# Four V stores on another queue and a reciprocal one step later, in a fused attention kernel

## The chip, the cores and the metric

The kernel runs on one core of a Trainium2 chip. The metric is the device time of one execution in microseconds; the median of three runs of the kernel before is 1255.03 (1254.48 to 1257.87).

## What is computed

Thirty-two sequences of 32 tokens with 512 channels pass a fused block: attention over a paged key and value cache (16 pages of 32 tokens per sequence) and the sequence's own new keys and values, a long convolution whose kernel is computed from state space parameters, a linear layer with a LoRA of each sequence, and a feed-forward part with gated low-rank experts. The change touches attention alone:

```python
q = rope(rmsnorm(einsum('bsd,ed->bse', x, Wq)))        # 32 heads of 128
k = rope(rmsnorm(einsum('bsd,ed->bse', x, Wk)))        # 8 heads
v = einsum('bsd,ed->bse', x, Wv)                       # 8 heads
k_all = concat([k_cache[block_table], k]); v_all = concat([v_cache[block_table], v])
scores = einsum('bqhd,bkhd->bhqk', q, k_all) * SCALE   # cached keys past the length masked
o = einsum('bhqk,bkhd->bqhd', softmax(scores), v_all)
x = x + conv(o @ Wo)
```

## The kernel before, in words

The work is done in two halves of 16 sequences (`HALVES`, loop variable h on every engine). A half is, in order: the projections of V's first four heads, K, Q and V's last four heads, twelve blocks of four tiles (128 tokens by 512 columns, each tile three passes of split float32 products, `tile`); the passage, in which the last V block is computed between the last transposes of Q; attention; the output projection and what follows. Each engine runs its own program; the order on it is written out by hand and held by semaphores.

**New keys and values.** K and V of the new tokens go through DRAM (`kn_d`, `vn_d`), since attention needs them in another layout. ScalarE (ACT) copies a V tile out of PSUM into a stage and, for the last four tiles (`col` 1, `store_v`, line 704), waits for its own copy and issues the store from its queue (lines 711 to 715). The first four tiles (`col` 0) are stored by SP (line 456). The stage of the last four has two slots, so the copy of tile m waits for the store of tile m-2. Both queues count in `vn_out`.

**SP's queue.** SP issues nearly all loads in one fixed order: keys' pages of batch 0, weights, at line 510 a wait for the last projection block but one, the first 8 key pages of batch 1, V's 16 pages of batch 0 (line 523, with a wait every four pages), key pages 8 to 15 and the new keys of batch 1, the wait for all V stores (line 525), both batches' new values (line 480), V's pages of batch 1 (line 485), and then per batch 16 key pages (line 470), new keys (line 475), new values and 16 V pages.

**Attention.** A batch is one sequence with 8 key heads g; the four query heads of a key head times 32 tokens are the 128 rows of a step. A step of each engine, for head g:
- TensorE (`attend`): scores of g, with key and query split in two parts (lines 1084 to 1095; L1090 is the first matmul that takes the keys' remainder `kbuf_lo`; every fourth head takes whole float32 instead, lines 1072 and 1074), transposes of the probabilities of g-3 (line 1107) into PSUM bank 4, products with V of g-4 (line 1139). Twice per batch the new tokens follow (lines 1119 and 1149), so that L1149 marks half-batches of four heads.
- VectorE (`step`, line 1622): masked maximum of g (line 1636) with its accumulator read, copy of the transposed probabilities of g-3 from PSUM (line 1642), a wait for ScalarE's exponential of g, reciprocal of the row sum of g (line 1649), and for g 1 and 5 `lower_q` (line 1595), the remainder of the next four query heads. TensorE may not transpose into bank 4 again before the copy (`pt_main`).
- ScalarE: high part of the keys of g+2 (line 815), exponential of g with the row sum (line 856), copies.
- GpSimd (POOL), `lower_keys`: per head g the keys' remainder of g (line 630, three heads of four), then `scale_probs(g-2)` (lines 616 and 618), which waits for the reciprocal (`rinv_ready`) and makes the probabilities ready to be transposed. The order is fixed: the remainder of the next keys stands behind the scale of the head before.

## Time and profile before

| | us |
|---|---|
| median of three runs | 1255.03 |
| the profiled execution, its time | 1256.73 |
| its span, first to last instruction | 1254.8 |
| TensorE busy in it | 1228.1 (98%) |
| VectorE, ScalarE, GpSimd busy | 808.2, 788.1, 749.5 |
| mean DMA rate | 171 GB/s |

The granted TensorE clock was 1.000 over the whole span. Matmul busy times are modelled and overlap, so 98% says that TensorE seldom stands, not that it is at its peak. The profile's chain is followed back from the last instruction; "SPq" in it is SP's queue issuing DMAs, "issue" is time in which nothing that the profile shows was waited for. PEld is TensorE's load of weights, which runs ahead of the matmul that uses them.

### The profile page before, as it was taken

How to read it: one execution, taken by the hardware profiler on the slowest of the kernel's cores; microseconds unless marked ns; L12 is line 12 of the kernel's file. 1: busy time of each engine (PE TensorE's matmuls, PEld its weight loads, DVE VectorE, ACT ScalarE, POOL GpSimd, SP SyncE). 2: the span in 40 equal slices, each digit the busy share in tenths (PEclk: the TensorE clock that was granted, in tenths of full speed). 3: DMA queues.
4: the chain of work that ended last, by engine and by line, in shares of the span. 5: the costliest groups of instructions: out<-in, count | busy, mean ns of one | idle time of the engine just before them, and what ended most of it. 6: DMA issues, size and time to landing. Idle time of an engine off the chain costs nothing.

```text
span 1254.8 us, 28770 instructions
## 1 busy us (share of the span) xinstructions
PE 1228.1 (98%) x7378; PEld 1031.9 (82%) x7378; DVE 808.2 (64%) x1736; ACT 788.1 (63%) x2259; POOL 749.5 (60%) x884
## 2 busy tenths in 40 slices
PE   7999999999999999999999999999999999999998
PEld 6788888899999997865777888888999999888756
DVE  6976666667666778951459667666766676655422
ACT  5666677778777774432346666777777777744320
POOL 4343467888888875433233443788888888844320
PEclk9999999999999999999999999999999999999999
DMA  6524288998999955306135252998899999534300
GB/s 206 194 92 149 95 232 220 230 232 233 236 236 237 229 159 177 142 8 194 68 105 184 84 172 91 243 220 227 224 234 240 231 238 239 121 116 153 89 30 34
DMA packets 147978, 214.82 MB, mean 171 GB/s; under 512 B 24949, under 2 KB 119479, under 8 KB 142136
## 3 DMA queue, kind: packets, MB, share of 16 engines
q1 hardware_dynamic: 134792, 206.96, 60.2%
q10 hardware_dynamic: 13104, 6.94, 1.9%
q8 instruction: 30, 0.49, 0.2%
q14 instruction: 52, 0.43, 0.1%
HBM read 203.33 MB, written 10.49 MB: 170 GB/s over the span
## 4 chain that ended last, share of the span: by engine, by line
PE 74%; SPq 15%; issue 5%; DVE 3%; ACT 1%; DMA 1%; ACTq 0%; DVEq 0%
PE PS L1139 12%; PE PS L1107 6%; SPq L485 6%; SPq L470 6%; PE PS L1206 5%; PE PS L1197 5%; PE PS L1001 5%; PE PS L1203 5%; PE PS L1005 5%; PE PS L999 5%; PE PS L1149 3%; PE PS L1248 2%; PE PS L985 2%; PE PS L1072 2%; PE PS L1237 1%
## 5 line engine op out<-in xcount | busy, mean ns | idle before, releaser
L630 POOL TENSOR_TENSOR kv_parts<-kv,k_hi 128x544 fp32r<-128x544 f32 x192 | 258.4, 1346 | 59.9 <-ACT k_hi L815 59.7
L1139 PE MATMUL PS<-probT,kv 128*128 128x128 f32 x2048 | 270.3, 275 | 0.0
L590 POOL TENSOR_TENSOR ring_parts<-ring,kv_parts 128x512 fp32r<-128x512 f32 x96 | 126.0, 1318 | 209.9 <-ACT kv_parts L693 181.6
L1139 PEld LDWEIGHTS PS<-probT,kv 128*128 128x128 f32 x2048 | 248.8, 192 | 0.0
L856 ACT ACTIVATE ring<-ring,smin 128x544 f32<-128x544 f32 x192 | 142.9, 744 | 86.9 <-DVE smin L1636 86.6
L1642 DVE COPY probT<-PS 128x512 f32<-128x512 f32 x256 | 175.5, 686 | 5.4 <-PE PS L1107 5.4
L1636 DVE CUSTOM_DVE_ANT_0 ring<-PS,mask,rq 128x544 f32<-128x544 f32 x192 | 149.7, 780 | 38.2 <-PE PS L1095 28.7
L652 POOL TENSOR_TENSOR ring_parts<-ring,kv_parts 128x512 fp32r<-128x512 f32 x64 | 85.0, 1332 | 95.1 <-ACT kv_parts L906 95.1
L815 ACT ACTIVATE k_hi<-kv 128x544 fp32r<-128x544 f32 x192 | 124.6, 650 | 15.5 <-DMA kv<-k_new 9.6
L618 POOL TENSOR_SCALAR ring<-ring,rinv 128x512 f32<-128x512 f32 x192 | 133.1, 693 | 0.0
L1676 DVE TENSOR_TENSOR qo_parts<-qo,kv_parts 128x512 fp32r<-128x512 f32 x64 | 85.3, 1339 | 54.1 <-ACT kv_parts L914 51.5
L1107 PE MATMUL PS<-consts,ring 128*128 128x128 f32 x768 | 115.8, 273 | 3.2 <-DVE probT L1642 2.4
L616 POOL TENSOR_SCALAR ring<-ring,rinv 128x32 f32<-128x32 f32 x192 | 79.6, 415 | 62.3 <-DVE rinv L1649 62.3
L1649 DVE RECIPROCAL rinv<-rsum 128x1 f32<-128x1 f32 x254 | 41.6, 164 | 114.7 <-ACT ring L856 95.6
L999 PE MATMUL PS<-kv_parts 128*128 128x512 f32 x352 | 102.3, 411 | 3.1 <-ACT kv_parts L693 1.5
L1206 PE MATMUL PS<-qo_parts,kv_parts 128*128 128x512 f32 x256 | 101.9, 398 | 0.0
L1197 PE MATMUL PS<-kv_parts 128*128 128x512 f32 x256 | 101.9, 398 | 0.0
L1203 PE MATMUL PS<-kv_parts,ring_parts 128*128 128x512 f32 x256 | 100.2, 392 | 0.0
L906 ACT ACTIVATE kv_parts<-ring 128x512 fp32r<-128x512 f32 x64 | 40.2, 631 | 94.5 <-PE PS L1197 94.4
L1107 PEld LDWEIGHTS PS<-consts,ring 128*128 128x128 f32 x768 | 89.8, 140 | 8.1 <-DVE probT L1642 3.3
L1001 PE MATMUL PS<-kv_parts 128*128 128x512 f32 x352 | 95.2, 392 | 0.0
L1005 PE MATMUL PS<-ring_parts,kv_parts 128*128 128x512 f32 x352 | 94.8, 391 | 0.0
(218 smaller groups left out, 2743.9 us busy)
## 6 DMA issues: line engine op xcount, KB each, us to landing
kv<-in_kpages SPq DMA_DIRECT2D x512, 128.0 KB, 2.5
kv<-in_vpages SPq DMA_DIRECT2D x512, 128.0 KB
ring<-in_w SPq DMA_DIRECT2D x44, 1024.0 KB, 5.0
k_new<-kv ACTq DMA_DIRECT2D x16, 256.0 KB, 2.3
kv<-k_new SPq DMA_DIRECT2D x32, 128.0 KB, 2.5
kv<-v_new SPq DMA_DIRECT2D x32, 128.0 KB
kv<-in_xT SPq DMA_DIRECT2D x8, 256.0 KB, 5.2
ring<-in_w SPq DMA_DIRECT2D x8, 256.0 KB, 5.4
```

What stands on the lines that cost most here:

```text
L630: nc.gpsimd.tensor_tensor(kbuf_lo(par)[:, :, g, :], kbuf(par)[:, :, g, :], k_hi[:, e % 2, :].rearrange("p (j t) -> p j t", t=PSIZE), ALU.s ...
L856: nc.scalar.activation(a, a, ACT.Exp, scale=-1.0, bias=smin[:, g:g + 1], accum_out=rsum[:, g:g + 1]).then_inc(exp_done, 1)
L999: nc.tensor.matmul(dst, x_hi[:, c, ms], hi[:, c, :], start=(c == 0), stop=False)
L1001: nc.tensor.matmul(dst, x_lo[:, c, ms], hi[:, c, :], start=False, stop=False)
L1005: mm = nc.tensor.matmul(dst, x_hi[:, c, ms], lo[:, c, :], start=False, stop=(c == KC - 1))
L1107: mm = nc.tensor.transpose(PS[:, 2048 + c * P:2048 + (c + 1) * P], prob(g % PRING)[:, c * P:(c + 1) * P], ident)
L1139: mm = nc.tensor.matmul(PS[:, at:at + D], vbuf(bpar)[:, c, gg * D:(gg + 1) * D], probT[:, g % 2, c * P:(c + 1) * P], start=(c == 0 and a = ...
L1197: mm = nc.tensor.matmul(bank(c), whi[:, a, cs], ohi[:, a, :], start=(head == 0), stop=False)
L1203: nc.tensor.matmul(bank(c), w[:, cs], ohi[:, a, :], start=False, stop=False)
L1206: mm = nc.tensor.matmul(bank(c), whi[:, a, cs], o, start=False, stop=(head == HQ - 1))
L1636: V.tensor_tensor_reduce(prob(g % PRING)[:, 0:LK], PS[:, at:at + LK], mask[:, par, :], rq[:, par, g:g + 1], 3.0e38, ALU.add, ALU.min, smin ...
L1642: V.tensor_copy(probT[:, (g - 3) % 2, :], bank(4)).then_inc(pt_main, 1)
```

## The change

Two edits. First, the stores of V's last four tiles move from ACT's queue to SP's: three between the V pages of batch 0 (after pages 3, 7 and 11), the fourth behind the new keys of batch 1 and directly ahead of SP's wait for all V stores. `store_values` now serves both columns. Second, in VectorE's step the reciprocal of a row sum moves: the one of head g-1 stands behind the masked maximum of g and ahead of the copy, and `lower_q` stands behind the copy.

```diff
@@ SP @@
+                def store_values(col, m, order):
+                    sp.wait_ge(v_read, h * (2 * TILES) + col * TILES + order + 1)
+                    sp.dma_start(vn_d[ds(h * HB + 4 * m, 4), :, col * D:(col + 1) * D]
+                                 .rearrange("b (t a) d -> (b t) a d", a=GU),
+                                 v_stage(col, m).rearrange("p (a d) -> p a d", a=GU)).then_inc(vn_out[m % 2], 16)
+
+                for order, m in enumerate((2, 3, 0, 1)):
+                    store_values(0, m, order)
...
                     load_value_page(0, j, pages[j])
+                    if j % 4 == 3 and j < NPP - 1:
+                        store_values(1, j // 4, j // 4)
+                        sp.sem_inc(sp_past, 1)
...
                 load_key_pages(1, pages, 8, NPP)
                 load_new_keys(1, 1)
+                store_values(1, 3, 3)
                 for n in range(2):
                     sp.wait_ge(vn_out[n], 8 * KU * (h + 1))
@@ ACT @@
-                    if col == 0:
-                        return
-                    act.wait_ge(v_read, h * (2 * TILES) + TILES + m + 1)
-                    act.dma_start(vn_d[ds(h * HB + 4 * m, 4), :, D:2 * D]
-                                  .rearrange("b (t a) d -> (b t) a d", a=GU),
-                                  v_stage(1, m).rearrange("p (a d) -> p a d", a=GU))\
-                        .then_inc(vn_out[m % 2], 16)
@@ VectorE, step @@
+                    if g <= HK and not (first and g == 0):
+
+                        k = (g - 1) % HK
+                        dve.wait_ge(exp_done, s)
+                        V.reciprocal(rinv[:, k:k + 1], rsum[:, k:k + 1]).then_inc(rinv_ready, 1)
                     if not (first and g < 3):
                         dve.wait_ge(pt_ready, s - 2)
                         if not (first and g < 5):
                             dve.wait_ge(pv_done, s - 4)
                         V.tensor_copy(probT[:, (g - 3) % 2, :], bank(4)).then_inc(pt_main, 1)
-                    if first and g == 1:
-                        dve.wait_ge(exp_done, s)
-                        V.reciprocal(rinv[:, 0:1], rsum[:, 0:1]).then_inc(rinv_ready, 1)
-                    if g < HK and not (first and g == 0):
-
-                        dve.wait_ge(exp_done, s + 1)
-                        V.reciprocal(rinv[:, g:g + 1], rsum[:, g:g + 1]).then_inc(rinv_ready, 1)
-                        if g % GU == 1:
-                            nb, u = (b, 1) if g == 1 else ((b + 1) % HB, 0)
-                            dve.wait_ge(qhi_ready, h * (QUADS + 1) + b * UNITS + g // GU + 2)
-                            dve.sem_inc(dve_past, 1)
-                            lower_q(u, ds(nb * (HQ * SEQ) + u * GU * D, NS * D))
+                    if g < HK and g % GU == 1:
+                        nb, u = (b, 1) if g == 1 else ((b + 1) % HB, 0)
+                        dve.wait_ge(qhi_ready, h * (QUADS + 1) + b * UNITS + g // GU + 2)
+                        dve.sem_inc(dve_past, 1)
+                        lower_q(u, ds(nb * (HQ * SEQ) + u * GU * D, NS * D))
```

## Rows read from the trace of the kernel before

**Rows 1.** The page, part 4: shares of the span on the chain that ended last.

```profile
PE 74%; SPq 15%; issue 5%; DVE 3%; ACT 1%; DMA 1%; ACTq 0%; DVEq 0%
```

**Rows 2.** The chain in order of time, 146 to 240 us: start, length, what.

```profile
148.69 0.98 SPq L463
...
177.91 1.62 SPq L485
...
233.76 2.43 DMA kv<-k_new
```

**Rows 3.** The same chain, 773 to 925 us (half 1), where it leaves SP.

```profile
915.53 2.86 DMA kv<-k_new
```

**Rows 4.** Line 456, SP's stores of V's first tiles: issue to landing.

```profile
DMA to landing us min/median/max: 2.6/2.7/2.9
```

**Rows 5.** Line 712, ACT's stores of V's last tiles: issue to landing.

```profile
DMA to landing us min/median/max: 3.2/3.9/5.4
```

**Rows 6.** Timeline of SP, 171 to 182 us: start, length, line, operation, count.

```profile
171.76 1.52 SPq L480 DMA_DIRECT2D kv<-v_new  x2
```

**Rows 7.** Timeline of TensorE's matmuls, 146 to 182 us; in brackets idle time and releaser.

```profile
165.68 0.40 PE L1090 MATMUL PS<-kv_parts,q_hi 128*128 128x288 f32 x1 [0.64 <-POOL kv_parts L630]
```

**Rows 8.** Timeline of VectorE, 413 to 421 us.

```profile
415.40 0.78 DVE L1636 CUSTOM_DVE_ANT_0 ring<-PS,mask,rq 128x544 f32<-128x544 f32 x1 [0.44 <-PE PS L1095]
...
416.11 0.69 DVE L1642 COPY probT<-PS 128x512 f32<-128x512 f32 x1
417.10 0.16 DVE L1649 RECIPROCAL rinv<-rsum 128x1 f32<-128x1 f32 x1 [0.31 <-ACT ring L856]
417.50 0.56 DVE L1595 TENSOR_TENSOR q_lo<-qo,q_hi 128x384 fp32r<-128x384 f32 x1 [0.24 <-issue]
417.98 0.78 DVE L1636 CUSTOM_DVE_ANT_0 ring<-PS,mask,rq 128x544 f32<-128x544 f32 x1
...
418.68 0.68 DVE L1642 COPY probT<-PS 128x512 f32<-128x512 f32 x1
```

**Rows 9.** Timeline of POOL, 413 to 421 us.

```profile
415.55 0.29 POOL L616 TENSOR_SCALAR ring<-prob,rinv 128x32 f32<-128x32 f32 x1
415.81 0.70 POOL L618 TENSOR_SCALAR prob<-prob,rinv 128x512 f32<-128x512 f32 x1
417.46 0.67 POOL L616 TENSOR_SCALAR ring<-ring,rinv 128x32 f32<-128x32 f32 x1 [0.95 <-DVE rinv L1649]
...
418.77 1.34 POOL L630 TENSOR_TENSOR kv_parts<-kv,k_hi 128x544 fp32r<-128x544 f32 x1
```

**Rows 10.** Timeline of TensorE's weight loads, 404 to 424 us.

```profile
411.44 0.19 PEld L1090 LDWEIGHTS PS<-kv_parts,q_hi 128*128 128x128 f32 x1
...
414.76 0.19 PEld L1095 LDWEIGHTS PS<-k_hi,q_lo 128*128 128x128 f32 x1
...
416.98 0.47 PEld L1107 LDWEIGHTS PS<-consts,ring 128*128 128x128 f32 x4
...
419.48 0.42 PEld L1107 LDWEIGHTS PS<-consts,prob 128*128 128x128 f32 x4 [0.27 <-issue]
...
421.01 0.19 PEld L1090 LDWEIGHTS PS<-kv_parts,q_hi 128*128 128x128 f32 x1
```

**Rows 11.** Timeline of TensorE, line 1149: one per half-batch, far apart in attention.

```profile
250.64 1.02 PE L1149 MATMUL PS<-kv 128*128 128x512 f32 x2
...
260.13 0.59 PE L1149 MATMUL PS<-kv 128*128 128x512 f32 x1
...
461.31 1.02 PE L1149 MATMUL PS<-kv 128*128 128x512 f32 x2
...
1085.74 0.59 PE L1149 MATMUL PS<-kv 128*128 128x512 f32 x1
```

**Rows 12.** Timelines of VectorE and POOL, 147 to 185 us: `lower_q` beside a scale.

```profile
166.43 0.61 DVE L1595 TENSOR_TENSOR q_lo<-qo,q_hi 128x384 fp32r<-128x384 f32 x1
...
165.94 0.69 POOL L618 TENSOR_SCALAR prob<-prob,rinv 128x512 f32<-128x512 f32 x1
```

More of the change, by code:

```diff
@@ L453, in _ @@
             with sp.Fori(0, HALVES) as h:
-                for k, m in enumerate((2, 3, 0, 1)):
-                    sp.wait_ge(v_read, h * (2 * TILES) + k + 1)
-                    sp.dma_start(vn_d[ds(h * HB + 4 * m, 4), :, 0:D].rearrange("b (t a) d -> (b t) a d", a=GU),
-                                 v_stage(0, m).rearrange("p (a d) -> p a d", a=GU)).then_inc(vn_out[m % 2], 16)
+                def store_values(col, m, order):
[5 more added lines that the diff above has]
+                    store_values(0, m, order)
                 with sp.Fori(0, 2) as i:
```

## The prediction

> **What bounds the kernel now.** I read the page's chain first. By engine it gives TensorE 74% of the span and SP's queue 15% [rows 1]: most of the run is matmul after matmul, but a sixth of it is SP issuing DMAs. Where does that lie? The chain in order of time shows one block per half: from 148.69, when SP reads the page table, it runs through SP's issues without a wait and leaves SP only at 233.76, with the landing of batch 4's new keys [rows 2]; in half 1 the block ends at 915.53 [rows 3]. From the passage into attention, up to batch 4 (half 0) or batch 7 (half 1), **SP's issue sequence sets the end**: what ACT, POOL or TensorE win there is lost again waiting for the next keys, and what SP loses there, the end loses. Behind that block attention is TensorE's: its half-batches (four heads) follow each other at (461.31 - 250.64) / 22 = 9.58 us [rows 11], the short ones at 9.49 (260.13 - 250.64). At most 0.09 of 9.58 is to be won.
>
> **Part 1: V's last four tiles stored by SP.** ACT loses four DMA issues and the waits on its own copies. SP gains, per half, three stores between V pages, one store behind `load_new_keys(1, 1)`, four waits on `v_read` and three increments.
> - ACT's side. Its third wait and issue stand before the key copy of head 2, so POOL's remainder of those keys comes late and TensorE stands 0.64 us at L1090 [rows 7]. Without them that stall goes, and perhaps as much again two heads on: 0.6 to 1.3 us a half. It lies inside SP's block, so I put it at **0**; it counts only if SP's block doesn't (rival D).
> - SP's issues. Two issues of like length (three-dimensional, L480) took 1.52 us [rows 6], 0.76 each. Three stores in the page loop: 3 x 0.75 = 2.25 us. Their waits I put at nothing: each has four page issues ahead of it, in which ACT makes the next copy. Queued behind them are V's pages of batch 0, the new values of both batches and all later keys and pages.
> - SP's new wait. The fourth store stands directly before the wait for `vn_out`, which wants all stores landed. Today ACT has issued the last one before SP is through with the second batch's keys, and no wait shows there. Now SP sits out a landing: 2.6 to 2.9 us for the stores of the projection [rows 4], 3.2 to 5.4 for those of this passage [rows 5]. I take 3.2 plus 0.1 of reaction, the low end of the nearer row (same place, busy DMA, but one store and not four). The landing holds the store's own issue.
> - What may come back: SP's issues sometimes stall, 1.62 us at 177.91 against some 0.4 for its neighbours [rows 2]. A queue that drained during the wait should not stall so soon; between 0 and 1.25, I take 0.4.
> - Sum: 2.25 + 3.3 - 0.4 = 5.2 us a half, **10.4 in all**. Bounds: 2.25 + 2.6 - 1.25 = 3.6 and 2.25 + 4.0 = 6.3 a half, 7 to 12.5 in all.
>
> The Trainium skill (DMA: Bandwidth & Descriptors, Issuing engines are not separate DMA queues) says that issuing from several engines only saves the sequencer's time, usually small. By that rule alone the part would be four issues, 3.0 us a half, and the forecast 4.4 us lower; it leaves out the landing.
>
> **Part 2: the reciprocal one step later.** Today VectorE does the masked maximum (L1636) and the copy of the turned probabilities (L1642), waits 0.3 us for ScalarE's exponential of the same head and takes the reciprocal (L1649); at heads 1 and 5 `lower_q` (L1595) follows [rows 8]. After: maximum of head g, reciprocal of g-1 with no wait, copy, and `lower_q` behind the copy. Two consequences, in times of the half-batch that starts at TensorE's load of L1090 for its first head, 411.44, and whose next starts at 421.01 [rows 10].
> - The copy comes later by the reciprocal, X, and TensorE's next transposes wait for it. For head 1: load of L1095 414.76, maximum 0.64 later (415.40), copy 0.71 after that, 0.69 long, and 0.12 to the load (418.68 + 0.68 to 419.48, a case that had to wait) = 2.16 + X, while TensorE itself is there 2.22 us after 414.76 (416.98). The slack is 0.06; behind head 3 I take 0.08. X is between 0.08 (the reciprocal's 0.16 less the 0.08 by which neighbours overlap: 417.98 against 417.50 + 0.56) and 0.40 (417.10 to 417.50, waits included) [rows 8]. The waits now stand behind an instruction of 0.78 us, which hides them, so I take 0.08: at most 0.03 a half-batch.
> - POOL gets the reciprocal of head g a step later. Today it scales head 0 at 415.55, stands, gets head 1's at 417.46, and that scale's first instruction takes 0.67 where 0.29 is usual [rows 9]: `lower_q` runs at 417.50. The two take turns. The other order is at 166.43: `lower_q` started beside a scale that ended at 165.94 + 0.69 = 166.63, and itself ended at 167.04, 0.41 behind it [rows 12]. After the change **the scale of head 0 and `lower_q` meet each time**. `lower_q` would start 0.08 + 0.69 - 0.08 = 0.69 behind reciprocal 0; POOL's long scale instruction starts 0.36 + 0.26 = 0.62 behind it and is first. The chain: L1090 of the first head to L1095 of head 1, 3.32; maximum 0.64; reciprocal of head 0, 0.71; POOL starts, 0.36 (417.10 to 417.46); both scale instructions 0.96 (415.55 to 416.51); `lower_q`'s 0.41 less 0.08 overlap; maximum of head 2, 0.71; reciprocal of head 1, POOL 0.36; its scale 0.93; then, in POOL's order, the remainder of the next keys, 1.34; TensorE 0.05. Sum 3.32 + 0.64 + 0.71 + 0.36 + 0.96 + 0.33 + 0.71 + 0.36 + 0.93 + 1.34 + 0.05 = **9.71**. Today that remainder starts at 418.77 and ends 0.9 us before its load at 421.01, which hides it; afterwards POOL sets the pace, 9.71 against 9.58. In SP's block that is hidden again (SP is slower still); outside it are 22 half-batches and a rest in half 0 and (1085.74 - 915.53) / 9.58 = 18 in half 1 [rows 3, 11]: 40 x 0.13 = **5.2 us** (0 to 10, for 0.12 either way in a chain of eleven terms).
>
> The Trainium skill (SBUF — State Buffer, SBUF: two separate sides) calls the port pair of VectorE and GpSimd an exclusive lock, held for a whole instruction, against a VectorE operation with two SBUF inputs, which `lower_q` is. By that rule the trace agrees in both directions, and the rule speaks against this change.
>
> **Sum.** The profiled execution took 1256.7 (span 1254.8). 1256.7 + 10.4 + 5.2 = 1272.3; the median of the runs shown is 1.7 lower than the profiled one, so **1271 us**.
>
> **Rivals.**
> - A, the forecast, chance 0.42: both costs hold; 1265 to 1277.
> - B, 0.20: SP's cost holds, but `lower_q` gets in ahead of the long scale (0.07 decides). Then 0.7 of the chain goes, and TensorE stays the bound at 9.49 to 9.58, on average 2 us less: 1255 + 10.4 - 2 = 1263 (1258 to 1268). For it: the margin is thin. Against: POOL's 0.36 is a steady figure and X can only be larger.
> - C, 0.12: POOL's cost holds, SP's is absorbed but for 1 us: 1255 + 5 + 1 = 1261 (1257 to 1264).
> - D, 0.20, **faster**: SP's additions vanish and attention doesn't suffer. It is decided by batch 2's keys: if they land no later than today in spite of four stores and a landing, because pages wait for the DMA engines (the issue of 1.62 us) and not for SP. Then ACT's relief counts, 2 x 1.3, and attention gives some of its 40 x 0.09: 1255 - 2.6 - 2 = 1250.5 (1249 to 1256). Against: the long issues would have to give back 5.5 us in one batch.
> - E, 0.06: X is 0.25: stalls of 0.19 and 0.17 on 9.49, 9.85 a half-batch, 40 x 0.27 = 11 beside SP's 10.4: 1276 (1273 to 1280).
>
> **How the numbers follow.** The likeliest is A. The range 1255 to 1277 leaves out most of D (0.16) and E's upper part (0.03). A measurement here tells about 0.3% from nothing, 3.8 us. Faster, below 1251.3: half of D and a little, 0.11. Within: the rest of D and C's lower edge, 0.11. Slower: 0.78.
>
> **What would show it.** SP: four `v_new` stores, a gap of 2.6 to 4 us before its first `v_new` load, the `k_new` load of batch 2 issued about 5 us later, and ACT's L815 or L1090 of batch 2 waiting that much longer. If the gap is there and batch 2 is not late, part 1 is wrong. Attention: no wait before reciprocals; `lower_q` drawn out to 0.8 to 1.0 us; L1090 of the first head of a half-batch waiting for POOL L630; half-batches of 9.7. If `lower_q` stays at 0.56 and TensorE doesn't wait for POOL, B is right; waits of L1107 for the copy at heads 1 and 3 would be E. Both halves must show the same.

## The result and the profile after

The changed kernel takes 1261.98 us (median of 6 runs, 1260.32 to 1264.34), beside 1256.71 us for the kernel before in the same rounds (1254.48 to 1257.87). The ratio is 1.0042, with a 95% interval of 1.0031 to 1.0054. It is slower by 5.3 us, which is more than a measurement can mistake; the forecast was 1271, some 15 us slower. The profiled execution of the changed kernel has a span of 1262.2 us at a mean granted clock of 0.997.

The page of the kernel after: a line of its first part, the chain by engine, and groups of instructions (busy time, mean ns of one, idle time before them and its releaser).

```profile
PE 1227.3 (97%) x7378; PEld 1039.6 (82%) x7378; DVE 783.4 (62%) x1736; ACT 788.4 (62%) x2259; POOL 747.1 (59%) x884
...
PE 71%; SPq 17%; issue 6%; DMA 2%; DVE 2%; ACT 1%; POOL 0%; ACTq 0%; DVEq 0%; POOLq 0%
...
L1140 PE MATMUL PS<-probT,kv 128*128 128x128 f32 x2048 | 271.5, 276 | 7.1 <-DMA kv<-in_vpages 6.8
...
L1637 DVE CUSTOM_DVE_ANT_0 ring<-PS,mask,rq 128x544 f32<-128x544 f32 x192 | 150.2, 782 | 173.3 <-PE PS L1096 112.0
...
L1648 DVE COPY probT<-PS 128x512 f32<-128x512 f32 x256 | 172.2, 673 | 5.5 <-PE PS L1108 5.5
...
L1108 PEld LDWEIGHTS PS<-consts,ring 128*128 128x128 f32 x768 | 91.0, 141 | 3.8 <-issue 2.1
```

TensorE's share of the chain has gone from 74% to 71%, SP's queue from 15% to 17%, DMA from 1% to 2% [rows 1]. Two new things are on this page. TensorE stands 6.8 us waiting for V pages, a wait that the kernel before does not list. And VectorE's idle time has moved. The page of before has

```profile
L1649 DVE RECIPROCAL rinv<-rsum 128x1 f32<-128x1 f32 x254 | 41.6, 164 | 114.7 <-ACT ring L856 95.6
```

and 38.2 us of idle time ahead of the masked maximum (L1636); now the two have 2.7 and 173.3 us. VectorE doesn't wait less, it waits at another place, ahead of the maximum. The weight loads behind the copy (L1107, L1108 after) do stand less, 3.8 us in the page's group where they stood 8.1. Most of their waits are these (before, and below the dots after: us in total, times, longest):

```profile
PEld PS L1107 <- issue: 15.8, 62, 0.3
...
PEld PS L1108 <- issue: 2.1, 8, 0.3
```

The row at 419.48 [rows 10] is one of the 62.

SP's timeline in the passage, half 0 (start, length, engine, line, operation, count):

```profile
157.19 0.60 SPq L456 DMA_DIRECT2D v_new<-kv  x1
...
161.24 0.55 SPq L456 DMA_DIRECT2D v_new<-kv  x1
...
164.61 0.57 SPq L456 DMA_DIRECT2D v_new<-kv  x1
...
168.68 3.99 SPq L474 DMA_DIRECT2D kv<-in_kpages  x8
172.87 0.39 SPq L479 DMA_DIRECT2D kv<-k_new  x1
173.52 0.59 SPq L456 DMA_DIRECT2D v_new<-kv  x1
177.93 1.50 SPq L484 DMA_DIRECT2D kv<-v_new  x2
179.64 7.58 SPq L489 DMA_DIRECT2D kv<-in_vpages  x16
```

Four stores, three between V pages and one behind the new keys, then nothing until 177.93: SP sits out the fourth one's landing. A landing is the time from a transfer's issue to its completion. The chain of the kernel after, 146 to 260 us and, below the dots, 773 to 925 us, says the same:

```profile
173.52 4.26 DMA v_new<-kv
...
802.06 3.47 DMA v_new<-kv
```

The first transfer behind the gap started at 171.76 before [rows 6] and starts at 177.93 now, 6.2 us later. TensorE, 178 to 196 us, where it waits for a DMA:

```profile
181.91 1.12 PE L1150 MATMUL PS<-kv 128*128 128x512 f32 x2 [1.71 <-DMA kv<-v_new]
194.26 1.16 PE L1140 MATMUL PS<-probT,kv 128*128 128x128 f32 x8 [3.51 <-DMA kv<-in_vpages]
```

So 5.2 us are spent waiting for the new values of batch 0 and the V pages of batch 1, and not, as forecast, for the keys of batch 2. Line 1150 (L1149 before) marks the half-batches. Its marks are 0.7, 4.5, 5.5, 5.4 and 4.7 us behind those of before for the first five, 4.3 behind at the eighth, and then the distance shrinks: the mark that was at 461.31 [rows 11] is at 464.90, 3.6 behind, and the one at 1085.74 [rows 11] at 1093.16, 7.4 behind. One slow transfer (at 304.19, 7.53 us from issue to landing) takes about 0.7 of the 3.6 in this execution. It is also where the chain leaves SP in half 0 (233.76 before [rows 2]), while in half 1 the chain leaves SP earlier than before, at 886.19 (915.53 before [rows 3]): the end of SP's block moves, and with it the number of half-batches that attention sets.

The shrinking is attention. VectorE, 410 to 422 us, and POOL, 410 to 422 us, the pair that answers to [rows 8] and [rows 9]:

```profile
410.74 0.16 DVE L1643 RECIPROCAL rinv<-rsum 128x1 f32<-128x1 f32 x1
410.81 0.67 DVE L1648 COPY probT<-PS 128x512 f32<-128x512 f32 x1
411.40 0.57 DVE L1596 TENSOR_TENSOR q_lo<-qo,q_hi 128x384 fp32r<-128x384 f32 x1
412.02 0.78 DVE L1637 CUSTOM_DVE_ANT_0 ring<-PS,mask,rq 128x544 f32<-128x544 f32 x1
...
420.82 0.55 DVE L1596 TENSOR_TENSOR q_lo<-qo,q_hi 128x384 fp32r<-128x384 f32 x1
```

```profile
411.13 0.29 POOL L624 TENSOR_SCALAR ring<-prob,rinv 128x32 f32<-128x32 f32 x1 [0.67 <-DVE rinv L1643]
411.39 1.06 POOL L626 TENSOR_SCALAR prob<-prob,rinv 128x512 f32<-128x512 f32 x1
...
413.35 0.69 POOL L626 TENSOR_SCALAR ring<-ring,rinv 128x512 f32<-128x512 f32 x1
...
420.93 0.99 POOL L626 TENSOR_SCALAR prob<-prob,rinv 128x512 f32<-128x512 f32 x1
```

The reciprocal has no wait in front of it (2.7 us in all 256), the copy starts 0.07 us behind it, and `lower_q` meets POOL's long scale as forecast. But `lower_q` keeps its plain 0.55 to 0.57 us and it is the scale that is drawn out, from 0.69 to 1.06. The maximum of the third head then starts as soon as it can (412.02), and the half-batches take 9.48 to 9.53 us instead of 9.49, 9.56, 9.55 and 9.72 in turn, whose mean is 9.58.

That is rival B, in both halves, with a time of 1262 against its 1263 (how much of that is luck is said below). What had to be found out: whether the two parts simply add, what a landing costs against an issue, why `lower_q` goes first, and whether the forecast's chain would have held if it had not.

### The profile page after: what moved, and what is told of

Same layout as the page of the kernel before. It is cut to its first block, busy times and chain, and to the rows that moved or that the text cites. A ratio compares the mean times of both kernels' runs of the same rounds, so it can differ in the third digit from the quotient of the medians.

```text
span 1262.2 us, 28776 instructions
## 1 busy us (share of the span) xinstructions
PE 1227.3 (97%) x7378; PEld 1039.6 (82%) x7378; DVE 783.4 (62%) x1736; ACT 788.4 (62%) x2259; POOL 747.1 (59%) x884
## 4 chain that ended last, share of the span: by engine, by line
PE 71%; SPq 17%; issue 6%; DMA 2%; DVE 2%; ACT 1%; POOL 0%; ACTq 0%; DVEq 0%; POOLq 0%
PE PS L1140 12%; SPq L489 7%; SPq L474 6%; PE PS L1108 6%; PE PS L1207 5%; PE PS L1198 5%; PE PS L1204 5%; PE PS L1006 5%; PE PS L1002 5%; PE PS L1000 5%; PE PS L1150 3%; PE PS L1249 2%; PE PS L986 2%; PE PS L1073 2%; SPq L467 1%
## 5 line engine op out<-in xcount | busy, mean ns | idle before, releaser
L1637 DVE CUSTOM_DVE_ANT_0 ring<-PS,mask,rq 128x544 f32<-128x544 f32 x192 | 150.2, 782 | 173.3 <-PE PS L1096 112.0
L1648 DVE COPY probT<-PS 128x512 f32<-128x512 f32 x256 | 172.2, 673 | 5.5 <-PE PS L1108 5.5
L1108 PE MATMUL PS<-consts,ring 128*128 128x128 f32 x768 | 116.4, 274 | 1.2 <-DVE probT L1648 0.8
L1108 PEld LDWEIGHTS PS<-consts,ring 128*128 128x128 f32 x768 | 91.0, 141 | 3.8 <-issue 2.1
L1554 DVE TENSOR_TENSOR kv<-PS,kv 128x512 f32<-128x512 f32 x80 | 55.2, 690 | 60.3 <-ACT prob L731 30.9
L1085 PE MATMUL PS<-k_hi,q_hi 128*128 128x288 f32 x192 | 92.2, 480 | 0.0
```

What stands on the lines that cost most here:

```text
L1108: mm = nc.tensor.transpose(PS[:, 2048 + c * P:2048 + (c + 1) * P], prob(g % PRING)[:, c * P:(c + 1) * P], ident)
L1637: V.tensor_tensor_reduce(prob(g % PRING)[:, 0:LK], PS[:, at:at + LK], mask[:, par, :], rq[:, par, g:g + 1], 3.0e38, ALU.add, ALU.min, smin ...
L1648: V.tensor_copy(probT[:, (g - 3) % 2, :], bank(4)).then_inc(pt_main, 1)
```

## Experiments

All were timed beside the kernel before in the same rounds. A time in brackets is the range of the runs.

### The stores alone

The kernel after, with the reciprocal put back (the order of VectorE's step as before).

> Part 1 alone: the four stores on SP, the reciprocal where it was. Theory S (the two parts add up; SP's later issues cost 4.5 us a half, attention gains 0.08 us per half-batch outside SP's block): 1256.7 + 9 = 1265 to 1266, batch 2's k_new load issued 4 to 5 us later than before, half-batches in late attention 9.49 to 9.72 as before. Rival T (the stores cost what the whole change cost, about 2.6 us a half, and the reciprocal does nothing): 1262. Rival U (the two parts need each other: SP's delay only hurts where VectorE no longer waits): 1257 to 1259.

1265.90 us (1265.62 to 1267.01), ratio 1.0067 [1.0054, 1.0080]: 9.1 us slower than the 1256.8 of before. The stall on TensorE is the same one:

```profile
181.36 1.12 PE L1150 MATMUL PS<-kv 128*128 128x512 f32 x2 [0.44 <-DMA kv<-v_new]
194.00 2.07 PE L1140 MATMUL PS<-probT,kv 128*128 128x128 f32 x8 [3.79 <-DMA kv<-in_vpages]
```

Its late half-batches keep the 9.58 us of before, and the distance of its marks stays at 4.3 us from the ninth to the end of half 0.

### The reciprocal alone

```
-                    if first and g == 1: ...
-                    if g < HK and not (first and g == 0): ...reciprocal of head g
+                    if g <= HK and not (first and g == 0): ...reciprocal of head g - 1, ahead of the copy
```

> Part 2 alone: the reciprocal behind the next maximum, V's stores as before on ACT. Theory S: 40 half-batches at 9.50 in place of 9.58 and the one late copy less behind SP's block, 1256.7 - 3.5 = 1253, with late half-batches of 9.48 to 9.53. My recorded forecast of this part (lower_q meets POOL's scale and waits): 1262, half-batches 9.7. Rival T (does nothing): 1256.7.

1253.21 us (1252.55 to 1254.07), ratio 0.9964 [0.9951, 0.9976]: 3.6 us faster. Marks of half-batches end half 0 at 1.4 us ahead of before, half 1 at 3.4 ahead; the late ones take 9.48 to 9.53 us. 9.1 - 3.6 = 5.5, against 5.3 measured for both (by the ratios 0.67% - 0.36% = 0.31%, against 0.42%, which the intervals cover): **the two parts add**, within about 1.5 us, and the theories in which one hides the other fall. The waits of L1107 are 2.1 us (8 times) here too, and 15.9 us (62 times) with the stores alone, so they belong to the reciprocal. No kernel of this study is faster than this one beyond the noise.

### The fourth store: on ScalarE again, or early

Two kernels split the price of the stores. In the first the kernel after has its fourth store back on ScalarE:

```
-                store_values(1, 3, 3)
                 for n in range(2):
                     sp.wait_ge(vn_out[n], 8 * KU * (h + 1))
...
+                    if col == 0 or m < 3:
+                        return
+                    act.wait_ge(v_read, h * (2 * TILES) + TILES + m + 1)
+                    act.dma_start(vn_d[...], v_stage(1, m)...).then_inc(vn_out[m % 2], 16)
```

> The changed kernel, but the fourth store stays on ACT's queue, so SP has no store directly ahead of its wait for all stores. Theory S (of SP's 5 us a half some 1.7 are the three issues, some 3.9 the wait for the last landing): two landings of 3.3 to 3.9 go, 1262 - 7 = 1255 to 1256, new values loaded right behind batch 1's new keys, batch 2's k_new some 1.5 to 2 us later than in the kernel before. Rival V (the landing is hidden, since pages wait for the DMA engines anyway, and it is the stores' issues that cost): 1261 to 1262.

1255.90 us (1254.89 to 1260.12), ratio 0.9996 [0.9984, 1.0007].

In the second all four are on SP, the fourth ahead of the eight key pages instead of behind the new keys:

```
+                store_values(1, 3, 3)
                 load_key_pages(1, pages, 8, NPP)
                 load_new_keys(1, 1)
-                store_values(1, 3, 3)
```

> The changed kernel, but SP's fourth store stands before key pages 8 to 15 of batch 1, so that nine issues cover its landing; SP issues all four. Theory S: SP pays four issues and no landing, about 2.6 us a half instead of 5.3: 1262 - 5.4 = 1256 to 1258, no wait of SP for stores. Rival V: 1261 to 1262. Should it be as fast as the one with three stores on SP, the fourth issue costs nothing.

1257.63 us (1253.98 to 1259.67), ratio 0.9996 [0.9986, 1.0007].

Read upwards from the reciprocal alone, by the medians: three stores on SP cost 1255.9 - 1253.2 = 2.7 us, the fourth as an issue 1257.6 - 1255.9 = 1.7, and **waiting for its landing** 1262.0 - 1257.6 = 4.4. By the ratios it is 0.9996 - 0.9964, 4.0 us, for three and for four stores alike, so the fourth's issue isn't resolved, and it is 1.0042 - 0.9996, 5.8 us, for waiting for the landing, in both halves together. The place of one DMA issue, nine issues earlier, is worth half or more of the 9.1 us that the stores cost. The DMA engines show where it goes. Stretches of 5 us with the busy times of PE, PEld, DVE, ACT and POOL (instructions in brackets), granted clock, DMA share and GB/s (a packet counts whole where it starts, so a share can pass 1.00): one of before,

```profile
175.00:180.00 5.00, 5.00 (x41) 4.79 (x41) 3.73 (x10) 4.02 (x11) 4.01 (x7) 1.00 1.00 227
```

and three of after:

```profile
175.00:180.00 5.00, 5.00 (x41) 4.69 (x39) 3.31 (x12) 4.03 (x11) 4.07 (x6) 1.00 0.18 52
180.00:185.00 5.00, 3.29 (x23) 2.63 (x23) 1.55 (x5) 1.76 (x6) 2.72 (x4) 1.00 0.91 202
...
190.00:195.00 5.00, 1.49 (x13) 1.25 (x12) 1.46 (x4) 2.82 (x9) 3.99 (x5) 1.00 1.08 239
```

While SP waits, the engines fall from 227 to 52 GB/s; then they are full to 195 us, and TensorE (1.49 of 5 us) waits for their backlog: the first eight key pages issued from 188.9 us on land 3.3 to 3.7 us later, where before, from 183.9 on, they took 2.6 to 2.8. Over 150 to 200 us the kernel before moves 218 GB/s and the kernel after 199: 0.95 MB less, 4.0 us at the 239 GB/s of the busy stretch, beside the 4.5 us by which TensorE's second mark is late. With the fourth store early the same stretch, 175 to 180 us, still moves 162 GB/s, and with three stores on SP 178.

Behind the long wait the clock falls too. In the kernel after the stretch that follows is

```profile
195.00:200.00 5.00, 5.00 (x26) 3.96 (x26) 1.33 (x4) 0.50 (x1) 0.00 (x0) 0.66 0.69 219
```

TensorE had been busy for 1.49 of the 5 us before; now it works without a pause, but its granted clock is 0.66, a mean of its two levels, 2.4 and 1.2 GHz (it stands at the lower one from 195.4 to 198.7 us), and it gets through 26 matmuls where 41 are usual. Whether that costs anything at the end isn't shown. The half-batch in it takes 11.1 us, the same one 10.1 before; but it takes 11.2 us with three stores on SP and with the four one-piece transfers below, both at 1.00 throughout. And among the executions of the kernel before that were timed beside these experiments, 38 with a mean granted clock of 0.997 took 1257.1 us on average and 17 with 1.000 took 1257.1 too.

### Four more transfers: in SP's block, late, and in one piece

If empty DMA time is the price, four further issues in the block should cost little as long as the engines stay fed. The first kernel adds them to the reciprocal alone:

```
                 load_new_keys(1, 1)
+                for n in range(4):
+                    sp.dma_start(pad[:, n:n + 1], bass.AP(dls_d.tensor, 0, [[0, P], [1, 1]])).then_inc(extra, 16)
```

> The reciprocal moved as in the changed kernel, no store moved, and four more transfers of 512 bytes (128 times 4 bytes, the same tiny source) issued by SP right behind the transfer of the new keys of the second batch in the passage, in each half; SP does not wait for them before its end. Nothing is left out. It asks what an issue alone costs in SP's block, without a landing that SP waits for. Theory (SP's block sets the start of attention, each issue costs its place in the queue): 4 issues at 0.6 to 0.9 us each, 2.4 to 3.6 us a half, of which some 1 us is slack in front of the first transfer that TensorE waits for; 1.5 to 2.5 us a half, about 4 us in all, so about 1257 us, ratio 0.9995 (0.998 to 1.001). Rival (only the landing waits of the change cost, the issues are hidden): 1252 to 1254.5 us, ratio 0.996 to 0.9975. Rival 2: an issue costs its whole place with no slack, 1259 to 1260 us.

1261.35 us (1260.25 to 1262.26), ratio 1.0033 [1.0021, 1.0045]: 8.1 us more than the reciprocal alone, more than any theory allowed. Its timelines of SP and of TensorE and its stretches:

```profile
170.50 1.88 SPq L528 DMA_DIRECT2D pad<-in_dls  x4
...
193.79 1.16 PE L1144 MATMUL PS<-probT,kv 128*128 128x128 f32 x8 [3.15 <-DMA kv<-in_vpages]
...
170.00:175.00 5.00, 5.00 (x42) 4.79 (x42) 3.38 (x9) 3.55 (x9) 5.00 (x7) 1.00 0.39 113
175.00:180.00 5.00, 5.00 (x42) 4.80 (x41) 3.40 (x9) 4.38 (x11) 4.07 (x7) 1.00 0.67 141
```

SP lost 1.9 us to the issues, and the V pages of batch 1 were issued only 0.4 us later than in the reciprocal alone (174.28 against 173.87; this execution had been 1.5 us ahead); but the engines moved 113 and 141 GB/s where that kernel has 190 and 214. The four transfers of 512 bytes, cut into 128 pieces of 4, took 2.7 to 6.5 us to land (median 4.6), and the loads behind them were late with them. My choice of a "small" transfer was the fault: it is an experiment on pieces, not on issues. The control had them behind the loads of the fourteenth batch:

```
                         load_kv(bb * 2 + par, par)
+                    with sp.If(bb > 5):
+                        with sp.If(bb < 7): ...the same four transfers
```

> The same four transfers, but issued by SP behind the loads of the fourteenth batch of each half (the reciprocal moved as in the changed kernel, no store moved). Nothing is left out. Control for the run with the transfers in the block. Theory (an issue costs only where SP's queue is late): within 0.5 us of the reciprocal alone, 1252.5 to 1254 us, ratio 0.996 to 0.9972. Rival (the transfers cost by themselves, wherever they stand, through the DMA rings or SP's branches): as much as in the block, 1255 us or more.

1256.73 us (1255.36 to 1262.29, 11 runs), ratio 1.0004 [0.9993, 1.0014]: 3.5 us more than the reciprocal alone, so issued late they are not free either, as the rival said. The half-batch beside them takes 10.71 us instead of 9.48 in half 0; the rest I can't place, and the two branches in SP's loop were added along with the transfers. As a control it is spoilt. The transfers in one piece make the clean case:

```
                 load_new_keys(1, 1)
+                for n in range(4):
+                    sp.dma_start(pad[:, 16 * n:16 * n + 2], bass.AP(dls_d.tensor, 0, [[0, 1], [1, 2]])).then_inc(extra, 16)
```

> The reciprocal moved as in the changed kernel, no store moved, and four more transfers of 8 bytes in one piece, issued by SP right behind the transfer of the new keys of the second batch in the passage, in each half; SP does not wait for them before its end. Nothing is left out. The run with four transfers of 128 pieces of 4 bytes at this place lost 8.1 us to the reciprocal alone; its rows show 1.9 us more on SP in each half, but also the DMA engines at 0.39 and 0.67 of their time for 10 us and TensorE waiting 3.15 us for V pages. This run takes the pieces away and keeps the issues. Theory (the block is bound by the transfers: what costs is DMA time left empty, and an issue of SP costs only where the engines run dry): the DMA share over 170 to 180 us stays within 0.1 of the reciprocal alone, and the time within 1.5 us of it, 1252.5 to 1255 us, ratio 0.996 to 0.998. Rival (SP's issue time is the path: 1.9 us a half whatever is moved): 1256.5 to 1258 us, ratio 0.9995 to 1.001.

1255.62 us (1253.21 to 1257.74, 12 runs), ratio 0.9984 [0.9974, 0.9994]: 2.4 us more than the reciprocal alone, between the two ranges. SP gave 1.24 us to the issues (0.31 each, against 0.47 with the pieces), and TensorE shows a wait for V pages in neither half. The DMA share over 170 to 180 us is 0.63 (0.69 and 0.56) where the reciprocal alone has 0.78 (0.65 and 0.91), more than the 0.1 that the theory allowed: the engines did run emptier. So **an issue in this block costs about 0.3 us** (2.4 / 8; by the two intervals anything from 0.1 to 0.6), and the pieces of the other version cost the remaining 5.7. The rival gave 1256.5 because it took 1.9 us a half for the issues; with the 1.24 that they took here it gives 1253.2 + 2 x 1.24 = 1255.7, the time measured. So it is the rival's mechanism, SP's issue time, that fits this run. The order of sizes: such an issue 0.3; the issue of a store 0.45 to 0.67 (2.7 / 6 by the medians, 4.0 / 6 by the ratios); a landing waited for 2.2 to 2.9 a half.

### A later `lower_q`

The question was whether the forecast's chain would have given 9.71 us if `lower_q` had lost its place. First try, on the reciprocal alone, three memsets in front of it:

```
                         dve.sem_inc(dve_past, 1)
+                        for n in range(3):
+                            V.memset(pad[:, n:n + 1], 0.0)
                         lower_q(u, ...)
```

> The reciprocal moved as in the changed kernel, no store moved, and in front of every lower_q three memsets of 128x1 on VectorE into a tile that nothing reads. Nothing is left out. It asks whether the order of lower_q and the long part of GpSimd's scale is what decided the second half of the change. In the reciprocal-only run lower_q started 0.66 us behind the reciprocal and got in just ahead of GpSimd's long scale, which was drawn out to 1.06 us, and the late half-batches took 9.50 us. The memsets put lower_q some 0.2 us later (three times the 0.07 us from the reciprocal's start to the next start, rounded). Theory (the order was the failed step, the chain behind it was right): the long scale keeps the first place, lower_q waits for it or is drawn out, the masked maximum of the third head and with it the weight load behind it come late, and the late half-batches take about 9.7 us; 40 of them at 0.2 us each are 8 us, so about 1261 us, ratio 1.003 to the kernel before. Rival (the order does not matter, the chain of the forecast was wrong too): half-batches within 0.03 us of 9.50, time 1252 to 1255 us, ratio 0.996 to 0.998.

1253.27 us (1252.48 to 1254.25), ratio 0.9970 [0.9959, 0.9980], late half-batches 9.48 to 9.57. The rival's numbers, yet no evidence for it: the memsets ran beside other work and put `lower_q` at most 0.05 us later. Second try, one reciprocal of 256 columns in their place:

```
+                        V.reciprocal(pad[:, 1 + g % 4, :], pad[:, 0, :])
```

> The reciprocal moved as in the changed kernel, no store moved, and in front of every lower_q one reciprocal of 128x256 f32 on VectorE between tiles that nothing else reads. Nothing is left out. Three memsets at this place delayed nothing (they ran beside the copy), so this is the same question with a real dose: by its own trace the 128x1 reciprocal takes 0.16 us, and 256 columns are taken for 0.3 to 0.5 us. Theory (the chain of the forecast stands once lower_q is late, whoever holds the port): lower_q ends 0.3 to 0.5 us later, the masked maximum of the third head, which had 0.05 us behind it, starts as much later, TensorE's transposes of that head wait, and a late half-batch takes 9.6 to 9.8 us instead of 9.50; if lower_q also loses its place to the long scale, 9.9 us or more. Time 1257 to 1270 us, ratio 1.0 to 1.01. Rival (that masked maximum has room, and the forecast's 9.71 us was wrong by its chain and not only by the order): half-batches 9.48 to 9.55 us, 1252 to 1255 us, ratio 0.996 to 0.998.

1326.19 us (1325.68 to 1326.69), ratio 1.0543 [1.0527, 1.0558]. VectorE's timeline, 444 to 449 us:

```profile
445.42 1.74 DVE L1654 RECIPROCAL pad<-pad 128x256 f32<-128x256 f32 x1
447.07 0.49 DVE L1597 TENSOR_TENSOR q_lo<-qo,q_hi 128x384 fp32r<-128x384 f32 x1
447.49 0.77 DVE L1638 CUSTOM_DVE_ANT_0 ring<-PS,mask,rq 128x544 f32<-128x544 f32 x1
```

The dose is four times what I had taken it for (1.74 us, 6.8 ns a column), but it bears on the room: `lower_q` 1.65 us later (447.07 against 445.42) makes a half-batch of 10.76, 1.26 more than 9.50. If it delays one for one beyond its room, the room is 0.4 us; one dose doesn't show the slope. Here POOL's long scale ran its plain 0.70 us beside the reciprocal of 256 columns. Third try, 36 columns:

```
+                        V.reciprocal(pad[:, 1 + g % 4, 0:36], pad[:, 0, 0:36])
```

> The reciprocal moved as in the changed kernel, no store moved, and in front of every lower_q one reciprocal of 128x36 f32 on VectorE between tiles that nothing else reads. Nothing is left out. The run with 256 columns here had an operation of 1.74 us; 36 columns at its 6.8 ns each are 0.24 us. That puts lower_q 0.9 us behind the reciprocal of the row sum, where the forecast had it behind the start of GpSimd's long scale. Theory (the order was the failed step, what it said would follow was right): the long scale runs in its plain 0.69 us in front of every lower_q, lower_q gets in only at its end, some 1.1 to 1.3 us behind the reciprocal, the masked maximum behind it 0.2 to 0.5 us late, and the late half-batches take 9.6 to 9.75 us instead of 9.50; that times some 56 half-batches is 6 to 14 us, so 1259 to 1267 us, ratio 1.002 to 1.008. Rival (lower_q gets in at once, drawing the scale out whether it comes first or second, or its 0.36 us of room, from the run with 256 columns, takes the delay): half-batches 9.48 to 9.55 us, 1252 to 1256 us, ratio 0.996 to 0.999.

1261.45 us (1259.74 to 1263.41, 12 runs), ratio 1.0034 [1.0024, 1.0044]: 8.2 us slower than the reciprocal alone, and the late half-batches take **9.71 us in half 0 and 9.70 in half 1** on average. VectorE, POOL and TensorE's weight loads of this kernel, 408 to 422 us:

```profile
409.35 0.37 DVE L1654 RECIPROCAL pad<-pad 128x36 f32<-128x36 f32 x1
409.63 0.81 DVE L1597 TENSOR_TENSOR q_lo<-qo,q_hi 128x384 fp32r<-128x384 f32 x1
...
419.36 0.50 DVE L1597 TENSOR_TENSOR q_lo<-qo,q_hi 128x384 fp32r<-128x384 f32 x1
...
409.34 0.69 POOL L619 TENSOR_SCALAR prob<-prob,rinv 128x512 f32<-128x512 f32 x1
...
419.19 1.14 POOL L619 TENSOR_SCALAR prob<-prob,rinv 128x512 f32<-128x512 f32 x1
...
413.74 0.19 PEld L1091 LDWEIGHTS PS<-kv_parts,q_hi 128*128 128x128 f32 x1 [0.19 <-POOL kv_parts L631]
```

Both orders stand in one kernel. At 409.34 the scale has the port: it takes 0.69, `lower_q`, 0.29 us behind its start, is drawn out to 0.81, and at 413.74 TensorE waits for POOL's remainder of the keys (line 631, L630 before), as the forecast had it. At 419.19 `lower_q`, 0.17 us behind the scale's start, takes 0.50 and the scale 1.14. Over the whole execution `lower_q` meets the long scale 62 times: in the 16 where it starts up to 0.17 us behind it, it goes first; in the 46 where it starts 0.18 us or more behind, it waits.

The half-batches sort by it, which is the test wanted, inside one kernel. In each of the 16 half-batches where `lower_q` goes first, TensorE doesn't wait for POOL and the half-batch takes 9.48 to 9.50 us. In the late ones where it waits, TensorE's load at the first head waits 0.18 to 0.24 us for POOL each time and the half-batch takes 9.70 to 9.84 us, 9.78 on average. (The pad operation alone, 0.29 us, costs nothing: the first kind has it too.) Three of four are of the second kind, and 9.71 is the mean of both.

In the kernel after all 60 meetings lie between 0.12 ahead and 0.04 behind, and `lower_q` goes first in each. In the kernel before it meets POOL's short scale instruction instead, 64 times, between 0.20 ahead and 0.05 behind, and goes first in each as well.

### A later copy

Two kernels: the reciprocal alone with three memsets, or (below the dots) with a reciprocal of 256 columns, between the moved reciprocal and the copy. They ask how much room the copy has for X.

```
                         V.reciprocal(rinv[:, k:k + 1], rsum[:, k:k + 1]).then_inc(rinv_ready, 1)
+                        for n in range(3):
+                            V.memset(pad[:, ...], 0.0)
...
+                        V.reciprocal(pad[:, 1 + g % 4, :], pad[:, 0, :])
```

> The reciprocal moved as in the changed kernel, no store moved, and behind every reciprocal, in front of the copy that it now precedes, three memsets of 128x1 on VectorE into a tile that nothing reads. Nothing is left out. It asks how much room the copy of the transposed probabilities has, that is whether the 0.07 us that the reciprocal puts in front of it could be at the edge. Theory (the copy is close to the path: the forecast gave it less than 0.1 us): 0.2 us more in front of it shows on TensorE in each of the 8 heads of a batch as a wait of about 0.1 us, 0.4 us a half-batch, so half-batches of 9.9 us and a time of about 1269 us, ratio 1.010. Rival (the copy has 0.3 us or more of room): half-batches within 0.05 us of 9.50 and 1252 to 1256 us, but for what the later lower_q behind it costs; then the waits of TensorE's weight loads on the copy stay where they were and those behind the masked maximum alone grow.

1253.84 us (1251.16 to 1256.16), ratio 0.9971 [0.9959, 0.9984]. The copy started 0.10 us behind the reciprocal instead of 0.07: no effect, and too small a dose to have one.

> The reciprocal moved as in the changed kernel, no store moved, and behind every reciprocal, in front of the copy, one reciprocal of 128x256 f32 on VectorE between tiles that nothing else reads. Nothing is left out. The same question as with the three memsets, which had delayed the copy by 0.03 us only, with a dose of 0.3 to 0.5 us. Theory (the copy is within 0.1 us of the path, so the 0.07 us of the moved reciprocal was near an edge): TensorE waits some 0.2 to 0.4 us in each of 8 heads, a late half-batch takes 10.3 to 11 us, the kernel 1285 us or more, ratio above 1.02. Rival (the copy has room for that much, and the moved reciprocal never came near to costing anything): half-batches under 9.6 us, the kernel under 1258 us.

1469.52 us (1469.36 to 1469.95), ratio 1.1682 [1.1666, 1.1699]. Stretch of that kernel, 420 to 470 us:

```profile
420.00:470.00 50.00, 39.30 (x286) 33.92 (x286) 47.95 (x83) 30.35 (x75) 29.57 (x43) 1.00 0.68 171
```

VectorE is busy 47.95 of 50 us: with 1.73 us more for each head it has become the bound itself, and the number says nothing of the copy's room. **That stays open**: 0.03 us beyond the change costs nothing, and more than that wasn't tried at a useful size.

## Why the prediction was wrong in size and right in direction

- **SP's block sets the end of the passage: right; what sets its pace is open.** SP's issuing alone is not all of it. In the 5 us of the bubble the DMA engines fell from 227 to 52 GB/s, and what was late at TensorE (V pages of batch 1, 3.51 us) was late through their backlog. I had read the unbroken row of SP's issues as an engine that sets the pace and never looked at the DMA share beside it: 1.00 in that stretch of before, and 0.81 over 150 to 200 us. For a bubble both readings give nearly the same price, since a bubble in SP's issuing is one in the transfers too. The four small transfers part them, in both ways: in pieces, SP issued them in 1.9 us and they cost 4 us a half, so there it was the transfers; in one piece they cost 1.2 us a half, the 1.24 that SP spent on them.
- **Size of part 1: 10.4 forecast, 9.1 measured**, within its bounds of 7 to 12.5. The issues: 4.5 forecast (2 x 2.25) for three stores in each half, 2.7 measured (4.0 by the ratios); 0.75 us each was read from the spacing of two loads [rows 6], the stores take 0.55 to 0.60, and the second batch's new keys come 1.7 us later (172.87 against 171.20), not 2.25. The landing: 3.3 us forecast, 4.26 and 3.47 us on the chain (2.6, 2.8 and 4.3 the least, median and most of all its stores), so the low end of [rows 5] was too low in half 0; against the early fourth store 4.4 us (by the ratios 5.8) lie on the path, and with the fourth's issue 6.1, where the forecast had 2 x (3.3 - 0.4) = 5.8.
- **Where it stalls: wrong.** Batch 2's new keys are issued 4.7 us late (193.84 to 198.56), as said, but TensorE had already lost the time at batch 0's new values and batch 1's V pages. The forecast named the queue behind the wait correctly (pages of V, new values) and then looked only at the keys.
- **X, the copy's delay: right**, 0.07 us against 0.08. Rival E doesn't occur.
- **Part 2: the sign was wrong, -3.6 us measured for +5.2. This is the step that failed:** "POOL's long scale instruction starts 0.36 + 0.26 = 0.62 behind it and is first". Both halves of it fail. The 0.36 that rival B's paragraph calls a steady figure (0.36 or 0.37 us in 63 of the 64 cases of the kernel before) is 0.44 to 0.52 in 45 of the 60 meetings of the kernel after, and the long scale starts 0.70 to 0.78 us behind the reciprocal, `lower_q` 0.66: there `lower_q` is simply first. Why POOL starts later is open. In the other 15 the scale does start first, by 0.01 to 0.04 us in the records, much as forecast (0.07), and `lower_q` goes first all the same.
- **The rows of before could have told.** From [rows 12], where it started 0.49 behind and lost, I inferred the order for 0.07. But [rows 8, 9] had the nearer case, read as "the two take turns": `lower_q` at 417.50 starts 0.04 behind the short scale at 417.46, keeps its 0.56 us, and it is the scale that is drawn out, to 0.67. In 42 of the 64 meetings of that kernel `lower_q` starts 0.01 to 0.05 us behind, and it goes first in all of them. The Trainium skill (SBUF — State Buffer, SBUF: two separate sides) calls the port an exclusive lock for whichever starts first. The runs agree in that one operation keeps its plain length and only the other is drawn out, in every meeting, though by less than what the first had left (0.31 of 0.40 us at 409.63, 0.37 of 0.58 at 411.39); of who starts first the recorded starts are no witness within 0.2 us.
- **The chain behind that step: right in kind, 0.07 us short.** Where `lower_q` is made to lose its place, a half-batch takes 9.78 us, forecast 9.71, with the wait for POOL at the first head, also forecast. That the averages of that run, 9.71 and 9.70, meet the forecast is luck: every fourth half-batch in them is one of 9.48 in which `lower_q` went first. So is 1261.45 - 1256.71 = 4.7 us beside the forecast's 5.2; with all 40 half-batches at 9.78 it would be 8.
- **What replaced it**: the gain that rival B allowed as "2 us less on average" is 3.6. What went are the waits of the weight loads behind the copy (62 of some 0.25 us before, 8 after), which fits an engine that no longer waits for ScalarE's exponential between its copies; VectorE's own idle time only moved. A late half-batch takes 9.50 us on average instead of 9.58.
- **ACT's relief: it came, and was rightly put at nothing.** In half 0 TensorE's waits of 0.64, 0.54, 0.99 and 0.60 us (165.68 to 171.23) are 2.77 us in the kernel before, 1.59 with the stores alone and one of 1.84, at 169.01, in the kernel after: 0.9 to 1.2 us less, inside the forecast's 0.6 to 1.3. The stores alone still lose their 9.1, so the relief lies inside SP's block.
- **Luck in the rival's number.** Rival B's 1263 is 1255 + 8.4; measured are 1256.7 + 5.3. Its cost of the stores is 1.3 us too high, its gain 1.6 too low, and its start, the median of three runs, 1.7 too low, and the errors nearly cancel.
- **Chances.** B had 0.20, though the text said that 0.07 us decides it. Such a margin should have sent me to all 64 meetings in the trace of before, which speak for B; without them A and B deserved about the same chance.

## What to carry to other kernels

A store that must have landed before the next loads belongs as many issues ahead of that wait as its landing takes: here nine issues' distance took 4.4 us out of the price, while moving a store's issue to the busy queue cost about half a microsecond (0.45 to 0.67). Where a queue's issues run without a wait, read the DMA share of the same stretch before saying what bounds it. When two engines ask for a shared port within 0.2 us of each other, the starts in the records don't tell who goes first: look up every meeting of the two in the trace at hand, see which was drawn out, and price both orders. And where an experiment's average meets a forecast, look at the single cases that it is the average of.

## What the runs showed that I had not expected

- The order at the port of VectorE and POOL turns within 0.01 us: in the run with 36 columns `lower_q` went first in all 16 meetings up to 0.17 us behind the recorded start of the scale and waited in all 46 from 0.18 us on (0.91 us long at 0.18, 0.81 at 0.29). It isn't a fixed figure: in the run with memsets ahead of the copy one of 59 `lower_q` started 0.08 us behind and waited, 1.02 us long, and why is open.
- POOL's scale isn't drawn out by every operation of VectorE: beside a reciprocal of 256 columns it took 0.70 us, beside `lower_q` 0.99 to 1.14.
- A f32 reciprocal on VectorE took 1.74 us for 256 columns and 0.37 for 36, that is 6.2 ns a column between the two and 0.15 us besides; the one of 128x1 moved here shows as 0.16 us and holds its neighbour back by 0.07; three memsets of 128x1 hold it back by 0.03.
- Four transfers of 512 bytes in 4-byte pieces, issued in 1.9 us, cost about 4 us a half, more than the waited-for landing of 256 KB; the same four in one piece 1.2.
- TensorE's granted clock fell to its lower level not only behind the longest waits. In the kernel after it did from 195.4 us on, behind a wait of 3.51 us, and from 799.5 on, behind one of 1.80 us, but not behind one of 2.80 us at 821.74. In the run with the pieces it stayed at 1.00 behind a wait of 3.15 us in half 0 and was at 0.50 from 820.1 to 826.8 us, around one of 2.93 us, in half 1. That such a fall lengthens the execution is not shown here.
